# Transposes of the feed-forward hidden tile in one PSUM bank instead of two in turn

## What is computed

```python
# x: (16, 2048, 1024) f32; 16 query heads, 4 key/value heads of 64, window 512
x = x + _layernorm(_L0_attn_ref(_layernorm(x), Wq, Wkv, Wproj))
x = x + _layernorm(_L0_ffn_ref(_layernorm(x), w1, b1, w2, b2))

def _L0_ffn_ref(x, w1, b1, w2, b2):           # w1: 1024 x 4096, w2: 4096 x 1024
    h = jax.nn.relu(jnp.einsum('bsd,dw->bsw', x, w1) + b1)
    return jnp.einsum('bsw,wd->bsd', h, w2) + b2
```

## Time and profile before

| | us |
|---|---|
| runs of the kernel, lowest to highest | 4559.95 to 4613.16 |
| their median (2 runs) | 4586.56 |
| the profiled execution, its own time | 4519.28 |
| its span on the slowest core (core 5) | 4517.7 |
| spans of the eight cores | 4503.2 to 4517.7 |
| stage B on core 5, from its first burst to the end of the span | 2822.75 to 4517.7 |

### The profile page before, as it was taken

One profiled execution on the slowest core, in us unless ns is written; L12 is line 12 of the kernel. 1 busy time (PEld: TensorE's weight loads), 2 busy tenths in 40 slices (PEclk: granted clock), 3 DMA queues, 4 the chain that ended last, 5 costly groups with the idle time before them and its releaser, 6 DMA issues.

```text
span 4517.7 us, 50405 instructions; the slowest of 8 cores (4503.2 to 4517.7 us)
## 1 busy us (share of the span) xinstructions
PE 2558.4 (57%) x15808; PEld 1310.1 (29%) x15808; DVE 1711.4 (38%) x4530; ACT 1259.9 (28%) x4001; POOL 9.4 (0%) x21
## 2 busy tenths in 40 slices
PE   2455455545544444545544553777767767776776
PEld 1123233323322122223323332333333333332332
DVE  2334333333333433333333342333433343334333
ACT  1344344444434344344434443000000000000000
POOL 0000000000000000000000000000000000000000
PEclk7565666666666656656666655888888988888888
DMA  8000000000000000000000013000000000000000
GB/s 137 19 10 10 19 10 10 10 19 10 10 19 10 12 17 10 15 14 10 10 19 10 10 29 75 19 19 19 19 19 19 19 27 21 19 19 19 19 19 19
DMA packets 20724, 93.13 MB, mean 21 GB/s; under 512 B 2336, under 2 KB 2352, under 8 KB 19056
## 3 DMA queue, kind: packets, MB, share of 16 engines
q1 hardware_dynamic: 18432, 67.12, 4.3%
q0 software_dynamic: 2032, 22.79, 3.0%
HBM read 78.89 MB, written 33.55 MB: 25 GB/s over the span
## 4 chain that ended last, share of the span: by engine, by line
PE 45%; DVE 23%; issue 12%; ACT 8%; DVEq 5%; DMA 4%; ACTq 2%; SPq 0%; POOL 0%; POOLq 0%
PE psO L728 6%; DVE sb_aT L582 6%; PE psX L728 5%; PE pjq L367 5%; DVEq L811 5%; PE pjq L643 4%; PE psAV L600 4%; PE ptr L572 3%; PE psE L709 3%; DMA sb_xt<-x 3%; PE pjk L709 3%; PE pjq L709 3%; DVE sb_st L253 3%; ACT sb_junk L524 2%; ACTq L811 2%
## 5 line engine op out<-in xcount | busy, mean ns | idle before, releaser
L572 PE MATMUL ptr<-sb_ident,sb_E 128*128 128x128 bf16 x2240 | 295.8, 283 | 724.3 <-DVE sb_aT L582 721.2
L276 PE MATMUL ptr<-sb_ident,sb_ln 128*128 128x128 bf16 x512 | 64.8, 307 | 637.6 <-DVE sb_ln L270 593.4
L572 PEld LDWEIGHTS ptr<-sb_ident,sb_E 128*128 128x128 bf16 x2240 | 182.0, 122 | 817.1 <-issue 807.6
L600 PE MATMUL psAV<-sb_aT,sb_VR 128*64 128x128 bf16 x2240 | 323.2, 300 | 86.3 <-DVE sb_aT L582 85.7
L582 DVE COPY sb_aT<-ptr 128x640 bf16<-128x640 bf16 (+4 forms) x720 | 263.1, 365 | 241.6 <-PE ptr L572 215.9
L696 PE MATMUL ptr<-sb_ident,sb_hT 128*128 128x128 bf16 x512 | 115.3, 225 | 358.0 <-DVE sb_hT L699 267.0
L728 PE MATMUL psO<-sb_warena,sb_hT 128*128 128x512 bf16 x1024 | 276.6, 437 | 0.0
L600 PEld LDWEIGHTS psAV<-sb_aT,sb_VR 128*64 128x64 bf16 x2240 | 214.5, 154 | 182.3 <-issue 176.7
L262 ACT ACTIVATE sb_st<-sb_st,sb_epsc 128x1 f32<-128x1 f32 x128 | 37.7, 294 | 796.2 <-DVE sb_st L258 796.2
L709 PE MATMUL pjq<-sb_warena,sb_lt 128*128 128x512 bf16 x1024 | 239.3, 382 | 1.3 <-DVE sb_lt L282 1.3
L276 PEld LDWEIGHTS ptr<-sb_ident,sb_ln 128*128 128x128 bf16 x512 | 49.6, 139 | 656.5 <-issue 656.5
(11 more groups left out here) (127 smaller groups left out, 4608.2 us busy)
## 6 DMA issues: line engine op xcount, KB each, us to landing
sb_xt<-x SPq DMA_DIRECT2D x32, 512.0 KB, 4.2
sb_warena<-w POOLq DMA_DIRECT2D x8, 2048.0 KB, 46.7
x1s<-sb_x1t SPq DMA_DIRECT2D x32, 512.0 KB, 2.9
sb_x1t<-x1s SPq DMA_DIRECT2D x32, 512.0 KB, 3.9
y<-sb_xt SPq DMA_DIRECT2D x32, 512.0 KB, 2.9
sb_warena<-wq POOLq DMA_DIRECT2D x1, 2048.0 KB, 26.4
sb_warena<-wp POOLq DMA_DIRECT2D x1, 2048.0 KB, 38.2
sb_warena<-wkv POOLq DMA_DIRECT2D x1, 1024.0 KB, 14.0
```

What stands on the lines that cost most here:

```text
L572: E("pe", lambda e, eb=eb, jj=jj, slot=slot: e.transpose(ptr[:, slot * 128:(slot + 1) * 128], eb[:, jj * 128:(jj + 1) * 128], ident[:]), r ...
L600: first=(jj == 0), last=(jj == len(chunks) - 1): e.matmul(outap, vap, atb[:, jj * 128:(jj + 1) * 128], start=first, stop=last, tile_positi ...
```

## The change

`trelu` uses the bank `ptr` alone, with eight column slots in turn in place of four slots in each of two banks. Instructions, their number, their shapes and their order are otherwise the same on every engine. Two reads of environment variables (Q0MODE, KVQMASK) go out as well; with their default values they selected nothing, so no instruction depends on them.

```diff
-            psAVb = psAV[:, :].bitcast(BF16)
             def trelu(m):
-                slot = (m // 2) % 4
-                if m % 2 == 0:
-                    bap, btg = ptr[:, slot * 128:(slot + 1) * 128], "ptr"
-                else:
-                    bap, btg = psAVb[:, slot * 128:(slot + 1) * 128], "psAV"
-                E("pe", lambda e, m=m, bap=bap: e.transpose(
-                    bap, hTb[:, m * 128:(m + 1) * 128], ident[:]),
-                  reads=(f"{hTt}_{m}", "ident"), writes=(btg,))
-                E("dve", lambda e, m=m, bap=bap: e.tensor_scalar(
-                    hTb[:, m * 128:(m + 1) * 128], bap,
+                slot = m % 8
+                E("pe", lambda e, m=m, slot=slot: e.transpose(
+                    ptr[:, slot * 128:(slot + 1) * 128],
+                    hTb[:, m * 128:(m + 1) * 128], ident[:]),
+                  reads=(f"{hTt}_{m}", "ident"), writes=("ptr",))
+                E("dve", lambda e, m=m, slot=slot: e.tensor_scalar(
+                    hTb[:, m * 128:(m + 1) * 128], ptr[:, slot * 128:(slot + 1) * 128],
                     b1f[:, m:m + 1], 0.0, OP.add, OP.max),
-                  reads=(btg, "b1f"), writes=(f"{hTt}_{m}",))
+                  reads=("ptr", "b1f"), writes=(f"{hTt}_{m}",))
```

More of the change, by code:

```diff
@@ L363, in q_half @@
             def q_half(half):
-                import os
-                q0mode = os.environ.get("Q0MODE", "full")
                 for c in range(8):
@@ L372, in q_half @@
                       reads=(lttag, "w_q"), writes=("pjq0",))
-                if q0mode == "mmonly":
-                    return
                 E("act", lambda e, half=half: e.activation(
@@ L377, in q_half @@
                   reads=("pjq0",), writes=("sqr", "q0tok"))
-                if q0mode == "nocopy":
-                    return
                 E("dve", lambda e, half=half: e.tensor_copy(
@@ L423, in qT_tr @@
                 transposes("qr", lambda c: qr[:, c * 128:(c + 1) * 128], 8, qTtag, qTb)
[L425 to L429, removed]
+            return [kv_mms, k_chain, kT_tr, lambda: q_half(0), lambda: q_half(1),
+                    q_chain, qT_tr]
         def tile_A(s, t, glob, nxt=None):
```

## The result

| | kernel before | changed kernel |
|---|---|---|
| median of the runs, us | 4519.98 (10 runs) | 5125.65 (11 runs) |
| lowest to highest, us | 4514.43 to 4638.38 | 5099.92 to 5165.9 |
| profiled execution: span, us | 4517.7 | 5120.5 |

In some executions of these kernels the cores of one die run at a lower clock and take some 2% longer (one of the kernel before took 4618.02 us, with 0.685 to 0.687 on the cores of one die and 0.718 or 0.719 on the others); the ratios and their intervals leave these out. The ratio is 1.1325, 95% interval 1.128 to 1.1369: slower by 13%, some 605 us by the medians. The forecast was 5175 us, with a range of 5040 to 5265.

What follows compares the result with a forecast made beforehand. Bound: the chain PE burst, cast, first relu, second transpose pair, next burst. Turns 342 plus clock 285 make 627 us, giving 5146 on 4519.28 or 5214 on 4586.56; forecast 5175, range 5040 to 5265.

Steps and rivals of the forecast that it cites:

- The turns: Stage B's loop and tail: each transpose waits for the previous relu, 0.75 us a turn; 10.7 us a tile, 342 us.
- some 500 us or more: Sign in stage B: transposes' idle time until a relu ends rises from 267.0 us, with about 800 waits.
- The clock: Stage B: longer pauses lower PE's clock, slowing burst matmuls (7.7 us) and transposes (1.2); 8.9 us a tile, 285 us.
- between 85% and all: Share of the 48 matmuls a tile in bursts 2 to 7 expected at the low level; 93%, 45, taken.
- Stage A's 85%: Share of stage A's matmuls at the low level, from line 367's mean of 596 ns; nearest kin to the changed loop.
- The low turns: Stage B: low-level transposes last 0.31 in place of 0.22 us; 0.05 us on each of 25 turns, 1.2 us a tile.
- The reference time: Whole kernel: base for the added 627 us; 4519.28 gives 5146, the median 4586.56 gives 5214, forecast between at 5175.
- The clock that stays up: Stage B's bursts keep the high level and only the turns count: 4861 us, or 4929 on the median; chance 8%.
- not slower: Stage B: next burst passes the waiting transposes, six groups cost nothing, low stretches shift off bursts; 4503 us, chance 2%.
- DVE sets the second half of a group: Loop: DVE, not the bank, already causes part of the waits; six groups cost half, clock stays up; 4737 us, chance 3%.

Runs made afterwards that it cites:

- two filled kernels: Extra 128x512 matmuls that nobody reads put in PE's waits: added to the changed kernel 4832.1 us, added to the kernel before 4498.05 us.
- The tail alone: Kernel before with one bank only for the last eight transposes of a tile, two banks in the loop: 4605.95 us, ratio 1.0192.
- batched kernel: Changed kernel, still one bank, with a group's four transposes issued together, then its four relus (eight and eight in the tail): 4245.54 us, ratio 0.9396.

## Why the prediction was right

*The turns.* Predicted 342 us, 10.7 a tile, from one turn of 0.75 us. Measured between the two filled kernels 334 us, 10.5 a tile. The tail alone cost 2.7 us a tile against 2.8. The count of waits (800, 25 a tile) came out as said, and the time in them (567.9 us) lay in what "some 500 us or more" allowed.

*The clock.* Predicted 8.9 us a tile, 285 us; measured 7.6 by the two filled kernels. By the groups, the matmuls that changed level are (599 - 482)/255 x 16 = 7.3 in `psE`, (571 - 414)/255 x 16 = 9.9 in `pjk` and (492 - 382)/255 x 32 = 13.8 in `pjq`, 31 a tile at 0.211 us, 6.5 us; the mean length of the bursts 2 to 7, 3.32 us after and 2.20 before, gives 6.7. I had 36, from 45 of 48 low; with the 8.7 that were low before it is 40 of 48, 83%. This is the mis-sized step: "between 85% and all", of which I took 93%. Stage A's 85% would have been the better number as it stood. The picture behind the number was off as well: I had the level stay low once it had fallen, with bursts of 3.62 us and a granted clock near 0.5 in the loop. It was 0.72 in the tile shown, the level often rose in a pause and fell again in the next burst, and just 99 of 192 bursts were low throughout.

*The low turns.* 0.80 against 0.75 us, the 0.05 that I took between 0 and 0.09. But only some 15 of a tile's 25 turns are of the longer kind: from one transpose to the next of its group it is 0.80 or 0.81 us 335 times in stage B, and 0.75 to 0.78 us 234 times. In the tile shown the short ones fall into stretches at 1.00 (3940.46 to 3941.22, 0.76 us). The term comes to 0.7 us where I had 1.2.

*Sum.* 6.5 to 6.7 for the matmuls, 0.7 for the longer turns and 10.5 for the turns make 17.7 to 17.9 us a tile, against 18.2 measured; what is left, up to half a us, I can't place. I had 19.6.

*The reference time.* The forecast stood between the profiled execution (4519.28) and the median of the two runs shown (4586.56). Ten runs put the kernel before at 4519.98, so the profiled execution was the right base: 4519 + 627 = 5146, 20 us from the result, where 5175 is 49 off. More than half of the miss is this choice. That 5146 comes so near is in part luck: the terms were too high by 1.4 us a tile, 45 us in all, and the 21 us ahead of stage B, which the slowest core of the changed kernel's profile had and no term foresaw, work the other way.

*Slips in the working.* By the prediction's own terms the ends of the range come to 4519 + 342 + 217 = 5078 and 4587 + 342 + 265 + 72 = 5266, where it says about 5090 and 5255; the stated range of 5040 to 5265 leaves no room above. The 1.27 us ahead of the next burst run from the end of the first pair of transposes (3526.72), not from the end of the burst. Neither decides anything here.

*The rivals.* The clock that stays up is refused by the changed kernel's rows and reproduced by filling the pauses. The kernel "not slower" would have needed the next burst to pass the waiting transposes; in the timelines shown it never does (the fourth transpose at 3929.60, the burst at 3929.66), and the tile is longer by the full turns. That DVE sets the second half of a group is refused by its idle time of 0.52 us in each turn.

## What to carry to other kernels

When two engines share a bank under one tag, the order of issue decides: a transpose and its reader one by one take turns at 0.75 us each, while four transposes and then four readers through the same bank cost no turn (PE waited for a relu twice in stage B of the batched kernel, 0.7 us in all on core 2, against 800 times and 567.9 us), and that was worth 880 us here. Price a new wait on PE twice, once as idle time and once by what it does to the granted clock of the matmuls behind it; here the second was almost three quarters of the first (7.6 and 10.5 us a tile). Where a profile shows PE's means between 379 and 634 ns for one shape, a few matmuls that nobody reads, placed in waits that end later than they do, tell at once what the clock costs.

## What the runs showed of the hardware that I had not expected

- Extra work made a kernel faster, and not by a little: 39 unread matmuls a tile took 294 us off the changed kernel, 30 a tile 117 us off the batched one. In a burst of eight, one matmul of 128x512 followed another after 0.427 us where the granted clock was 0.50 (3.62 us a burst), and after 0.216 us where it was 1.00 (1.89 us).
- The mean granted clock of a stretch can hide where it was low. The changed kernel's loop had 0.72 in the tile shown, yet by the means 83% of the matmuls of bursts 2 to 7 ran at the low level, 0.50: the level came back in pauses that hold a few transposes, and was gone again in the bursts behind them.
- The low clock lasts longer than its cause. In the batched kernel burst 3 of a tile, the second burst behind the long pause, still took 2.71 us in place of 1.89, and `pjk`, which serves bursts 3 and 7, had a mean of 428 ns; with the two long pauses filled it was 379.
